# Half visits between turned scores, turned values a column later, and the last group's root and scaled rows placed otherwise

## The chip, the cores and the metric

One core of a Trainium2 chip. The metric is device time in microseconds of one execution, median of three runs.

## The reference

A layer on 16 sequences of 256 channels by 512 positions: cross attention over the channels (8 heads of 32 channels, softmax with a scale from each sequence's token count), a residual, layernorm, and a mixture of 8 experts with top-2 routing and a capacity of 1280 rows, with a second residual.

```python
s = SCALE * jnp.log(k_length.astype(jnp.float32))[:, None, None, None]
attn = jnp.einsum('bhdq,bhdk->bhqk', qh, kh)
attn = jax.nn.softmax(s * attn, axis=-1)
out = jnp.einsum('bhqk,bhdk->bhdq', attn, vh)
...
x = x + _L0_xcond_ref(_layernorm(x, axis=-1), ctx_2048, ctx_2048, itok_B_779_1933)
x = x + _L0_ffn_ref(_layernorm(x, axis=-1), L0_ffn_Wg, L0_ffn_w1, L0_ffn_w2)
```

The expert layer takes the softmax of `xr @ Wg`, its two largest values and their experts, counts each expert's rows in order, drops rows past the capacity, runs relu(x w1) w2 for each expert on its rows and adds the two results with their gates.

## The kernel before, in words

The attention works on 32 groups of 128 channels (4 heads each). Every engine has its own program, written out by hand; semaphores tie them together. The scores of a group are computed twice: unturned (queries on partitions, `ps_s`, L1050), from which VectorE takes the row maxima (`nmax`, L668), and turned (keys on partitions, `ps_t`, L1003), with the maxima as two more rows of the stack, from which ScalarE takes the exponentials (`probs`, L447). Queries and keys are split into a high and a low part (`qhi`, `khi` on ScalarE, L515 and L439; `qlo`, `klo` on GpSimd, L402 and L393), which SyncE stacks by DMA (`qst`, `kst`).

A step s is a software pipeline over groups: unturned scores of group s, turned scores of group s - 2, in 4 columns c of 4 heads i, one of each kind in turn. In between stand "half visits" (`weighted`): products of probabilities and values (`products`, `ps_o`, L971) and row sums (`row_sums`, `ps_l`, L979) for two chunks; chunks 2 and 3 of group s - 3 behind column 0, chunks 0 and 1 of group s - 2 behind column 2. Ahead of column 2 stand four transposes of the scaled rows of group s - 5 (`row_turned`, L1010) and four of the context, which give the values (`values`, L1018, of group s - 1). Both go into the turned scores' banks; ScalarE copies them out (`x2t` L494, `vt` L454). Behind column 3 come the router's logits. There are three banks of each kind: score k waits until score k - 3 has been read (`s_free`, `t_free`). `bank_turns` gives the number of each use of a bank.

In odd steps from 7 on a pair of groups is routed: VectorE, between its maxima, forms gates (`pr` L703, two inputs), the token numbers (`xrow<-tok` L709, one input), the indices of the two largest (`topi` L717), `hot` (L721, two inputs) and counts. GpSimd does in each step, in this order: the root of the next group's variance (`st` L377, L380, L385), `klo`, the residual addition (`x` L330, `residual`), in even steps four indirect writes of rows to the experts' buffer (`dispatch`, L336), `qlo`, and a second root (`root2`, L367, L370).

After the steps come the last two groups' turned scores (g = 30 and 31) with the half visits, the transposes and the logits in between, on four banks; then, for the last two groups, rows scaled (`x_scaled` L573), turned, logits, experts picked, counted (`places`), and written (`dispatch_one`). `warm` issues matmuls whose result is not used. When all rows are written, the experts start; their part is PE bound and is not touched.

SyncE's program asks for `ct` (context, L269) of group s + 3 after the values of group s - 1 have been turned:

```python
if g >= 4:
    sp.wait_ge(t_done, t_turn["vt", g - 4])
    sp.wait_ge(klo_ready, g - 3)
sp.dma_start(ct[g % 4][:], by_dim(ctx_rows, g)).then_inc(c_ld[g % 4], 16)
```

Of the kernel before, what the change touches and what calls it, by code (L numbers as in the profile page):

```python
# [10 lines left out]
ALU = mybir.AluOpType  # L11
# [55 lines left out]
def bank_turns():  # L67

    s_turn, t_turn = {}, {}
    for s in range(SLOTS):  # L70
        for c in range(NC4):
            if c == 2 and live(s - 5):
                t_turn["x2t", s - 5] = len(t_turn) + 1
            if c == 2 and live(s - 1):
                t_turn["vt", s - 1] = len(t_turn) + 1
# [27 lines left out]
def attention_and_dispatch(nc, x_rows, ctx_rows, klen, wg, out_rows, disp, totals, fill, spare,  # L103
                           w1, w2, raw, raw_ld, xin, first_ld, ident):
    s_turn, t_turn, (s_main, t_main) = bank_turns()
    with ExitStack() as stack:
# [201 lines left out]
        def _(pool):  # L308
# [31 lines left out]

            def dispatch(i):
# [9 lines left out]
                rows_to_experts(2 * i)  # L351
                rows_to_experts(2 * i + 1)
# [11 lines left out]

            def root2(g):
                pool.wait_ge(var2, g + 1)
                nc.gpsimd.tensor_scalar(st2[g % 2][:, 8:9], st2[g % 2][:, 7:8], EPS, None, ALU.add  # L367
                                        ).then_inc(veps2, 1)
                pool.wait_ge(veps2, g + 1)
                nc.gpsimd.tensor_tensor(st2[g % 2][:, 9:10], st2[g % 2][:, 8:9], nhalf[:], ALU.pow  # L370
                                        ).then_inc(rstd2, 1)
# [53 lines left out]
            root2(G - 1)  # L425
# [6 lines left out]
        def _(act):  # L432
# [48 lines left out]
            for s in range(-2, SLOTS):  # L481
                for c in range(NC4):
# [12 lines left out]
                    if c == 2 and live(s - 1):  # L495
                        values(s - 1)
                    for i in range(HPG):
                        if live(s - 2):
                            powers(s - 2, c, i)
                        if (c, i) == (0, 2) and pair_in(s):  # L500
# [4 lines left out]
                            for h in range(2):  # L505
                                nc.scalar.activation(lexp[:, h, :], lg[n % 2][:, h, :], ACT.Exp, bias=lmax[:, h:h + 1]
                                                     ).then_inc(rt["lexp"], 1)
                    if c == 0 and live(s - 3):
                        sums_out(s - 3)
                    if c == 1 and s >= 0 and live(s + 2):  # L510
                        keys_high(s + 2)
                    if live(s + 2) and c == (1 if s < 0 else 3):
# [9 lines left out]
            for g in (G - 2, G - 1):  # L522
                for c in range(NC4):
                    powers(g, c, 0)
                    powers(g, c, 1)
                    if c == 0:
                        sums_out(g - 1)
                        row_turned(g - 3)
# [18 lines left out]
        def _(dve):  # L547
# [84 lines left out]
            for s in range(-2, SLOTS):  # L632
# [28 lines left out]
                for c in range(NC4):  # L661
                    for i in range(HPG):
# [29 lines left out]
                        if (c, i) == (0, 1) and live(s + 2):  # L692
# [200 lines left out]
            x_scaled(G - 1)  # L893
# [3 lines left out]
            nc.vector.tensor_tensor(last[:, 1, :], last[:, 0, :], picked[:, 0, :], ALU.add).then_inc(rt["before"], 1)  # L897
            gates_found(B, G - 2, 0, 1)
# [28 lines left out]
        def _(pe):  # L927
# [55 lines left out]
            def last_weighted():  # L983
                pe.wait_ge(t_free, t_turn["t", G - 1, NC4 - 1, HPG - 1])
                held = probs[(NC4 * G - 1) % NPROBS]
                for h in range(HPG):
                    hd = slice(HD * h, HD * h + HD)
# [833 lines left out]
```

## Time and profile before

| | |
|---|---|
| median of 3 runs | 2154.31 us (2147.97, 2154.31, 2155.99) |
| the profiled execution | 2153.56 us, its span 2151.8 us |
| TensorE (PE) busy | 2087.6 us (97%) |
| weight loads (PEld) busy | 1511.5 us (70%) |
| VectorE (DVE) busy | 1032.1 us (48%) |
| ScalarE (ACT) busy | 679.6 us (32%) |
| GpSimd (POOL) busy | 472.7 us (22%) |
| VectorE busy, 60 to 560 us | 446.32 of 500 us |
| TensorE busy, 60 to 560 us | 496.56 of 500 us |
| experts, from about 650 us | 1501.8 us, TensorE busy 1485.14 |

The first scores start at 24 us and end at 584; the last two groups' turned scores run to 625, the dispatch to 640. The odd step shown below begins at 317.4, the even one at 299.9; step 31 begins at 566.7. A row of a timeline gives start and duration; the duration of a matmul is longer than the distance to the next one, because they overlap. In brackets stands how long the engine (or the weight load, PEld) was idle before, and what ended it.

### The profile page before, as it was taken

Reading aid. Unit: us, or ns where it says so; the run is one execution under the profiler, and the core shown is the slowest. Engines: PE = TensorE matmul, PEld = TensorE weight load, DVE = VectorE, ACT = ScalarE, POOL = GpSimd, SP = SyncE. Lnnn points to the kernel's source line nnn. Section 1 sums busy time; section 2 is a strip of 40 time slices with the busy share of each in tenths; the row PEclk is TensorE's granted clock in tenths of the full one; section 3 lists DMA queues with packets and bytes.
Section 4 is the critical chain, followed back from the end, with each engine's and each line's share of the span. In section 5 each row is a group of like instructions: output and inputs, shape, how many; then the busy total and the mean of one; then the engine's idle time right before and its main releaser. Section 6 shows DMA issues by size and latency. Waiting matters only on the chain. (4 is left out here: it accounts for less than half of the span.)

```text
span 2151.8 us, 26863 instructions
## 1 busy us (share of the span) xinstructions
PE 2087.6 (97%) x10150; PEld 1511.5 (70%) x10150; DVE 1032.1 (48%) x1914; ACT 679.6 (32%) x1187; POOL 472.7 (22%) x591
## 2 busy tenths in 40 slices
PE   3999999999989999999999999999999999999997
PEld 1455555555557788878888888888887788888775
DVE  5788989898844343233324324423332342333211
ACT  1666666666533132122213212312211231221110
POOL 3334444444332103010310301111031011101101
PEclk9999999999999999999999999999999999999999
DMA  9877778777545426125322613622532252241101
GB/s 148 168 165 183 173 184 179 182 178 179 107 152 145 96 82 140 21 42 128 70 38 83 136 21 80 132 45 40 128 69 41 60 132 45 40 128 29 20 3 20
DMA packets 177962, 215.89 MB, mean 100 GB/s; under 512 B 33807, under 2 KB 105487, under 8 KB 177808
## 3 DMA queue, kind: packets, MB, share of 16 engines
q1 hardware_dynamic: 154128, 173.21, 34.5%
q0 software_dynamic: 22240, 37.92, 9.2%
q10 hardware_dynamic: 1440, 2.70, 0.5%
q8 instruction: 97, 1.59, 0.3%
q14 instruction: 57, 0.47, 0.1%
HBM read 113.93 MB, written 68.29 MB: 85 GB/s over the span
## 5 line engine op out<-in xcount | busy, mean ns | idle before, releaser
L1551 DVE SCALAR_TENSOR_TENSOR hlo<-ps_h,hhi 128x512 fp32r<-128x512 f32 x256 | 177.2, 692 | 937.4 <-ACT hhi L1428 901.5
L1428 ACT ACTIVATE hhi<-ps_h 128x512 fp32r<-128x512 f32 x256 | 153.7, 600 | 1128.4 <-PE ps_h L1692 1114.9
L1690 PE MATMUL ps_h<-xhi,w1hi 128*128 128x512 f32 x1024 | 405.0, 396 | 2.2 <-PEq L1277 1.3
L1709 PE MATMUL ps_y<-w2hi,hhi 128*128 128x512 f32 x1024 | 404.0, 394 | 1.5 <-issue 0.8
L1710 PE MATMUL ps_y<-w2lo,hhi 128*128 128x512 f32 x1024 | 404.0, 395 | 1.4 <-issue 1.4
L1691 PE MATMUL ps_h<-xlo,w1hi 128*128 128x512 f32 x1024 | 404.7, 395 | 0.0
L1692 PE MATMUL ps_h<-xhi,w1lo 128*128 128x512 f32 x1024 | 404.3, 395 | 0.0
L1711 PE MATMUL ps_y<-w2hi,hlo 128*128 128x512 f32 x1024 | 403.9, 394 | 0.0
L668 DVE TENSOR_REDUCE nmax<-ps_s 128x1 f32<-128x512 f32 x512 | 328.9, 678 | 62.1 <-PE ps_s L1050 54.3
L447 ACT ACTIVATE probs<-ps_t 128x512 f32<-128x512 f32 x504 | 266.5, 613 | 133.0 <-PE ps_t L1003 129.5
L1690 PEld LDWEIGHTS ps_h<-xhi,w1hi 128*128 128x128 f32 x1024 | 192.6, 188 | 50.0 <-issue 3.9
L1711 PEld LDWEIGHTS ps_y<-w2hi,hlo 128*128 128x128 f32 x1024 | 192.2, 188 | 47.7 <-issue 1.6
L1709 PEld LDWEIGHTS ps_y<-w2hi,hhi 128*128 128x128 f32 x1024 | 192.2, 188 | 47.3 <-DVE hlo L1551 1.2
L1710 PEld LDWEIGHTS ps_y<-w2lo,hhi 128*128 128x128 f32 x1024 | 192.3, 188 | 47.1 <-issue 1.0
L1692 PEld LDWEIGHTS ps_h<-xhi,w1lo 128*128 128x128 f32 x1024 | 192.7, 188 | 46.3
L1691 PEld LDWEIGHTS ps_h<-xlo,w1hi 128*128 128x128 f32 x1024 | 192.7, 188 | 46.1
L1050 PE MATMUL ps_s<-kst,qst 96*128 96x512 f32 x416 | 185.4, 457 | 30.2 <-DMA qst<-qlo 27.3
L1363 POOL DMA_INDIRECT out_x<-y,ids x64 | 103.5, 1617 | 455.5 <-DVE y L1593 441.5
L1003 PE MATMUL ps_t<-qst,kst 98*128 98x512 f32 x408 | 165.6, 409 | 5.4 <-DMA qst<-nturn 2.4
L1345 POOL TENSOR_TENSOR ids<-xtail,zeros 128x4 int32<-128x4 int32 x15 | 5.2, 347 | 714.2 <-DMA xtail<-dispatched 714.2
L1050 PEld LDWEIGHTS ps_s<-kst,qst 96*128 96x128 f32 x416 | 81.6, 197 | 106.3 <-issue 64.9
L971 PE MATMUL ps_o<-probs,vt 128*32 128x512 f32 x1016 | 122.7, 600 | 1.8 <-ACT probs L447 1.8
(194 smaller groups left out, 1967.1 us busy)
## 6 DMA issues: line engine op xcount, KB each, us to landing
raw<-in_L_ffn_w SPq DMA_DIRECT2D x128, 512.0 KB
qst<-qhi SPq DMA_DIRECT2D x64, 256.0 KB, 7.5
xin<-dispatched SPq DMA_DIRECT2D x60, 256.0 KB, 5.9
kst<-khi SPq DMA_DIRECT2D x52, 256.0 KB, 6.4
xt<-in_x SPq DMA_DIRECT2D x32, 256.0 KB, 3.0
ct<-in_ctx SPq DMA_DIRECT2D x32, 256.0 KB, 4.2
qst<-qlo SPq DMA_DIRECT2D x32, 256.0 KB, 8.2
xres<-in_x SPq DMA_DIRECT2D x32, 256.0 KB, 4.5
```

The costliest lines, as they stand in the source:

```text
L447: nc.scalar.activation(probs[n % NPROBS][:, i, :], t_at(k)[:], ACT.Exp).then_inc(t_free, 1)
L668: nc.vector.tensor_reduce(nmax[s % 2][:, i, c:c + 1], s_at(k)[:], AX, ALU.max, negate=True).then_inc(s_free, 1)
L1003: nc.tensor.matmul(bank[:], kst[g % KR][0:STACK + 2, i, cols], qst[g % KR][0:STACK + 2, i, :], start=True, stop=True).then_inc(t_done, 1)
L1050: nc.tensor.matmul(bank[:], qst[s % KR][0:STACK, c, cols], kst[s % KR][0:STACK, c, :], start=True, stop=True).then_inc(s_done, 1)
L1428: nc.scalar.activation(hhi[k % 2][:], ps_h[k % 3][:], ACT.Relu).then_inc(hhi_ready, 1)
L1551: nc.vector.scalar_tensor_tensor(hlo[k % 2][:], ps_h[k % 3][:], 0.0, hhi[k % 2][:].bitcast(F32), ALU.max, ALU.subtract).then_inc(h_ready, 1)
L1690: nc.tensor.matmul(to, w1hi[:, c, fs], xhi[n % 2][:, c, :], start=(c == 0), stop=False)
L1691: nc.tensor.matmul(to, w1hi[:, c, fs], xlo[n % 2][:, c, :], start=False, stop=False)
L1692: done = nc.tensor.matmul(to, w1lo[:, c, fs], xhi[n % 2][:, c, :], start=False, stop=(c == NC4 - 1))
L1709: nc.tensor.matmul(ps_y[b][:], hhi[k % 2][:, bs], w2hi[:, f, :], start=(f == 0), stop=False)
L1710: nc.tensor.matmul(ps_y[b][:], hhi[k % 2][:, bs], w2lo[:, f, :], start=False, stop=False)
L1711: done = nc.tensor.matmul(ps_y[b][:], hlo[k % 2][:, bs], w2hi[:, f, :], start=False, stop=(f == NF - 1))
```

## The change

Nothing is computed otherwise; instructions change places.

- Values (`values` on TensorE and their copy on ScalarE) stand ahead of column 3 instead of column 2, and `bank_turns` with them.
- On ScalarE `keys_high(s + 2)` (khi) moves from behind column 1 to behind column 0, ahead of `sums_out`; `qhi` from behind column 3 to behind column 2.
- On VectorE `q_stats(s + 2)` moves from behind maximum (0, 1) to behind (0, 3).
- In the last two groups every column gets half a visit, between its second and third turned score: row sums of chunks 2 and 3 of the group before, their products, products of chunks 0 and 1, their row sums. Chunks 2 and 3 of the last group both stand in `last_weighted`.
- `root2(G - 1)` moves into the dispatch of groups 28 and 29, between them; `x_scaled(G - 1)` behind the counts; `row_turned(G - 1)` behind `places(B)`.

```diff
@@ bank_turns, ScalarE and TensorE alike
-            if c == 2 and live(s - 1):
+            if c == 3 and live(s - 1):
                 t_turn["vt", s - 1] = len(t_turn) + 1
...
@@ dispatch (GpSimd)
                 rows_to_experts(2 * i)
+                if i == B - 2:
+                    root2(G - 1)
                 rows_to_experts(2 * i + 1)
...
             dispatch(B - 2)
-            root2(G - 1)
             dispatch_one(G - 2)
...
@@ ScalarE, steps
+                    if c == 0 and s >= 0 and live(s + 2):
+                        keys_high(s + 2)
                     if c == 0 and live(s - 3):
                         sums_out(s - 3)
-                    if c == 1 and s >= 0 and live(s + 2):
-                        keys_high(s + 2)
-                    if live(s + 2) and c == (1 if s < 0 else 3):
+                    if live(s + 2) and c == (1 if s < 0 else 2):
...
@@ ScalarE, last two groups
                     if c == 0:
+                        row_turned(g - 3)
+                    if c == 1:
                         sums_out(g - 1)
-                        row_turned(g - 3)
...
@@ VectorE
-                        if (c, i) == (0, 1) and live(s + 2):
+                        if (c, i) == (0, 3) and live(s + 2):
                             q_stats(s + 2)
...
             experts_picked(B, lg[(B - 1) % 2], 0, 1)
-            x_scaled(G - 1)
             experts_marked(B, 0, 1)
...
             nc.vector.tensor_tensor(last[:, 1, :], last[:, 0, :], picked[:, 0, :], ALU.add).then_inc(rt["before"], 1)
+            x_scaled(G - 1)
             gates_found(B, G - 2, 0, 1)
...
@@ TensorE, last_weighted
+                g = G - 1
+                pe.wait_ge(t_free, t_turn["t", g, 2, HPG - 1])
+                row_sums(g, (2,))
+                products(g, (2,))
+                pe.wait_ge(t_free, t_turn["t", g, 3, HPG - 1])
+                row_sums(g, (3,)).then_inc(l_done, 1)
+                products(g, (3,)).then_inc(pv_done, 2)
...
@@ TensorE, last two groups
                     if c == 0:
-                        weighted(g - 1, (2, 3))
+                        pe.wait_ge(t_free, t_turn["t", g - 1, 3, HPG - 1])
+                        row_sums(g - 1, (2, 3)).then_inc(l_done, 1)
+                    if c == 1:
+                        products(g - 1, (2, 3)).then_inc(pv_done, 2)
                     if c == 2:
-                        weighted(g, (0, 1))
-                    if c == 3 and g == G - 1:
-                        weighted(g, (2,))
+                        pe.wait_ge(t_free, t_turn["t", g, 1, HPG - 1])
+                        pe.wait_ge(t_free, t_turn["vt", g])
+                        pe.wait_ge(o_saved, g)
+                        products(g, (0, 1))
+                    if c == 3:
+                        pe.wait_ge(l_saved, g)
+                        row_sums(g, (0, 1)).then_inc(pv_done, 2)
...
-            row_turned(G - 1)
             pe.wait_ge(rt["counted"], B - 1)
             pe.wait_ge(rt["picked"], B)
             places(B, 0, 1)
+            row_turned(G - 1)
```

How the instructions move, first on ScalarE in an odd step, from the routing's exponentials of column 0 on. Before:

```order
L506 ACTIVATE lexp<-lg,lmax 128x8 x2
L447 ACTIVATE probs<-ps_t 128x512
L460 ACTIVATE o_sb<-ps_o 128x512
L447 ACTIVATE probs<-ps_t 128x512 x4
L439 ACTIVATE khi<-ct 128x512
L494 ACTIVATE x2t<-ps_t 128x512
L454 ACTIVATE vt<-ps_t 128x512
L447 ACTIVATE probs<-ps_t 128x512 x8
L515 ACTIVATE qhi<-qf 128x512
L447 ACTIVATE probs<-ps_t 128x512 x4
```

Now (the changed kernel's lines are numbered one or two apart):

```order
L507 ACTIVATE lexp<-lg,lmax 128x8 x2
L448 ACTIVATE probs<-ps_t 128x512
L440 ACTIVATE khi<-ct 128x512
L461 ACTIVATE o_sb<-ps_o 128x512
L448 ACTIVATE probs<-ps_t 128x512 x4
L495 ACTIVATE x2t<-ps_t 128x512
L448 ACTIVATE probs<-ps_t 128x512 x4
L516 ACTIVATE qhi<-qf 128x512
L455 ACTIVATE vt<-ps_t 128x512
L448 ACTIVATE probs<-ps_t 128x512 x8
```

The copy of the keys has moved from between the exponentials of column 1 and `x2t` to ahead of `o_sb`, the copy of the values behind column 2, and `qhi` ahead of it.

TensorE in group 30, from its column 0 to column 2 (`ps_l` and `ps_o` rows are the half visits). Before:

```order
L1003 MATMUL ps_t<-qst,kst 128x512 x2
L979 MATMUL ps_l<-probs,ones 32x512 x8
L971 MATMUL ps_o<-probs,vt 32x512 x8
L1010 MATMUL ps_t<-ident,xrow 128x128 x4
L1003 MATMUL ps_s<-qst,kst 128x512
L1003 MATMUL ps_t<-qst,kst 128x512 x3
L1026 MATMUL ps_s<-wg_sb,qf 128x8 x4
L1003 MATMUL ps_s<-qst,kst 128x512
L1003 MATMUL ps_t<-qst,kst 128x512 x3
L971 MATMUL ps_o<-probs,vt 32x512 x8
L979 MATMUL ps_l<-probs,ones 32x512 x8
L1018 MATMUL ps_s<-ident,ct 128x32x4 x4
```

Now:

```order
L1001 MATMUL ps_t<-qst,kst 128x512 x2
L981 MATMUL ps_l<-probs,ones 32x512 x8
L1008 MATMUL ps_t<-ident,xrow 128x128 x4
L1001 MATMUL ps_s<-qst,kst 128x512
L1001 MATMUL ps_t<-qst,kst 128x512 x3
L973 MATMUL ps_o<-probs,vt 32x512 x8
L1024 MATMUL ps_s<-wg_sb,qf 128x8 x4
L1001 MATMUL ps_s<-qst,kst 128x512
L1001 MATMUL ps_t<-qst,kst 128x512 x3
L973 MATMUL ps_o<-probs,vt 32x512 x8
L1016 MATMUL ps_s<-ident,ct 128x32x4 x4
L1001 MATMUL ps_t<-qst,kst 128x512 x3
```

Where 16 matmuls of a visit stood together, 8 stand between each two pairs of turned scores; the row sums of chunks 0 and 1 follow further down, in column 3.

GpSimd at the end, from the dispatch of groups 28 and 29 (`rowi` of 4 columns) on. Before:

```order
L347 TENSOR_TENSOR rowi<-rowd,zeros 128x4
L336 DMA dispatched<-xrow,rowi 10240x528 x4
L367 TENSOR_SCALAR st_1<-st_1 128x1
L370 TENSOR_TENSOR st_1<-st_1,nhalf 128x1
L360 TENSOR_TENSOR rowi<-rowd,zeros 128x2
L336 DMA dispatched<-xrow,rowi 10240x528 x2
L360 TENSOR_TENSOR rowi<-rowd,zeros 128x2
L336 DMA dispatched<-xrow,rowi 10240x528 x2
```

Now:

```order
L355 TENSOR_TENSOR rowi<-rowd,zeros 128x4
L336 DMA dispatched<-xrow,rowi 10240x528 x2
L343 TENSOR_SCALAR st_1<-st_1 128x1
L346 TENSOR_TENSOR st_1<-st_1,nhalf 128x1
L336 DMA dispatched<-xrow,rowi 10240x528 x2
L370 TENSOR_TENSOR rowi<-rowd,zeros 128x2
L336 DMA dispatched<-xrow,rowi 10240x528 x2
L370 TENSOR_TENSOR rowi<-rowd,zeros 128x2
L336 DMA dispatched<-xrow,rowi 10240x528 x2
```

The two instructions of the last group's root have moved ahead of two of the four row writes.

## Rows read from the trace of the kernel before

**Rows 1.** Timeline of TensorE, odd step: start, duration, what, count
```profile
325.16 0.63 PE L1010 MATMUL ps_t<-ident,xrow 128*128 128x128 f32 x4
325.65 0.63 PE L1018 MATMUL ps_t<-ident,ct 128*128 128x128 f32 x4
...
328.70 1.92 PE L971 MATMUL ps_o<-probs,vt 128*32 128x512 f32 x16
```

**Rows 2.** Timeline of TensorE, an even step, and step 31
```profile
307.69 0.63 PE L1010 MATMUL ps_t<-ident,xrow 128*128 128x128 f32 x4
...
310.98 1.92 PE L971 MATMUL ps_o<-probs,vt 128*32 128x512 f32 x16
...
574.51 0.63 PE L1010 MATMUL ps_t<-ident,xrow 128*128 128x128 f32 x4
...
577.99 1.93 PE L971 MATMUL ps_o<-probs,vt 128*32 128x512 f32 x16
```

**Rows 3.** Timeline of the weight loads, odd step, with what ended the idle time
```profile
327.05 0.19 PEld L1003 LDWEIGHTS ps_t<-qst,kst 98*128 98x128 f32 x1 [0.50 <-ACT x2t L494]
...
328.04 0.19 PEld L1050 LDWEIGHTS ps_s<-xin,qst 96*128 96x128 f32 x1 [0.33 <-DVE nmax L668]
```

**Rows 4.** Timeline of VectorE, odd step
```profile
326.03 0.16 DVE L703 TENSOR_TENSOR pr<-lexp,zinv 128x16 f32<-128x16 f32 x1
...
326.38 0.15 DVE L709 TENSOR_SCALAR xrow<-tok 128x2 int32<-128x2 f32 x1
...
328.51 0.71 DVE L721 TENSOR_TENSOR hot<-e_f,topi 128x32 f32<-128x32 f32 x1
```

**Rows 5.** Timeline of GpSimd, odd step
```profile
325.52 0.19 POOL L385 TENSOR_TENSOR st<-st,sharp 128x1 f32<-128x1 f32 x1
326.65 1.28 POOL L393 TENSOR_TENSOR klo<-ct,khi 128x512 fp32r<-128x512 f32 x1 [0.94 <-ACT khi L439]
327.89 1.28 POOL L330 TENSOR_TENSOR x<-o_sb,xres 128x512 f32<-128x512 f32 x1
```

**Rows 6.** One line's instructions, L721: count, duration in ns, min/median/max
```profile
L721 DVE TENSOR_TENSOR hot<-e_f,topi x13: 186/717/731, 149.4 to 577.8; 128x32 f32<-128x32 f32 x13
```

**Rows 7.** Timelines of VectorE and GpSimd at the kernel's start
```profile
10.22 1.10 DVE L642 CAST tok<-tok_i 128x32 f32<-128x32 int32 x1
...
10.02 1.26 POOL L402 TENSOR_TENSOR qlo<-qf,qhi 128x512 fp32r<-128x512 f32 x1 [1.02 <-ACT qhi L515]
```

**Rows 8.** Timeline of TensorE, group 30, values behind a half visit
```profile
599.96 0.66 PE L1018 MATMUL ps_s<-ident,ct 128*128 128x128 f32 x4
600.37 0.95 PE L1003 MATMUL ps_t<-qst,kst 98*128 98x512 f32 x3
```

**Rows 9.** Timeline of TensorE, group 30, the visit with chunks 0 and 1
```profile
594.69 3.18 PE L971 MATMUL ps_o<-probs,vt 128*32 128x512 f32 x16 [1.28 <-ACT probs L447]
597.63 2.40 PE L979 MATMUL ps_l<-probs,ones 128*32 128x512 f32 x16
```

**Rows 10.** Busy time by stretch: length, PE, PEld, DVE, ACT, POOL, granted clock, DMA, GB/s
```profile
596.00:597.00 1.00, 1.00 (x12) 0.36 (x8) 0.00 (x0) 0.00 (x0) 0.00 (x0) 0.50 0.99 371
...
584.00:626.00 42.00, 36.94 (x255) 16.97 (x255) 20.57 (x79) 20.74 (x44) 13.50 (x21) 0.96 0.38 134
```

**Rows 11.** Timelines of VectorE, GpSimd and TensorE, last group's variance, root and rows
```profile
628.63 0.18 DVE L786 BATCH_NORM_AGGREGATE st<-st 128x2 f32<-128x6 f32 x1
...
630.20 0.25 POOL L367 TENSOR_SCALAR st<-st 128x1 f32<-128x1 f32 x1
...
631.74 0.66 PE L1010 MATMUL ps_t<-ident,xrow 128*128 128x128 f32 x4 [0.77 <-DVE xrow L573]
```

**Rows 12.** SyncE's load of ct, ScalarE's fourth exponential of the next step, landing of ct loads
```profile
314.21 0.62 SPq L269 DMA_DIRECT2D ct<-in_ctx  x1
...
320.29 0.59 ACT L447 ACTIVATE probs<-ps_t 128x512 f32<-128x512 f32 x1
...
DMA to landing us min/median/max: 3.0/4.2/4.7
```

More of the change, by code:

```diff
@@ L339, in rows_to_experts, with root2 @@
                         bounds_check=E * CAP - 1, oob_is_err=False).then_inc(row_st[g % RING], 16)
+            def root2(g):
+                pool.wait_ge(var2, g + 1)
+                nc.gpsimd.tensor_scalar(st2[g % 2][:, 8:9], st2[g % 2][:, 7:8], EPS, None, ALU.add
+                                        ).then_inc(veps2, 1)
+                pool.wait_ge(veps2, g + 1)
+                nc.gpsimd.tensor_tensor(st2[g % 2][:, 9:10], st2[g % 2][:, 8:9], nhalf[:], ALU.pow
+                                        ).then_inc(rstd2, 1)
             def dispatch(i):
@@ L363, in dispatch_one @@
                 rows_to_experts(g)
[L365 to L371, printed above, removed]
             for s in range(-2, SLOTS):
@@ L494, in _ @@
                         nc.scalar.activation(x2t[:], t_at(k)[:], ACT.Copy).then_inc(t_free, 1)
-                    if c == 2 and live(s - 1):
+                    if c == 3 and live(s - 1):
                         values(s - 1)
@@ L983, in last_weighted @@
             def last_weighted():
[L984 to L987, printed above, removed]
-                    done = nc.tensor.matmul(ps_l[hd, :], ones[:, 0:HD], held[:, h, :], start=False, stop=True)
-                done.then_inc(l_done, 1)
-                for h in range(HPG):
-                    hd = slice(HD * h, HD * h + HD)
-                    done = nc.tensor.matmul(ps_o[hd, :], vt[(G - 1) % 4][:, NC4 - 1, hd], held[:, h, :],
-                                            start=False, stop=True)
-                done.then_inc(pv_done, 1)
+                g = G - 1
[5 more added lines that the diff above has]
+                products(g, (3,)).then_inc(pv_done, 2)
             def turned_logits(g, c, i):
@@ L1041, in _ @@
                         row_turned(s - 5)
-                    if c == 2 and live(s - 1):
+                    if c == 3 and live(s - 1):
                         values(s - 1)
```

## The prediction, made before the changed kernel ran

> **What bounds the kernel now.** I read the page first, then the timeline engine by engine. The page has TensorE busy nearly throughout, and the reader should not take that for a floor: a busy matmul row also covers short waits for a bank. From about 650 us on the experts run, and the change does not touch them. So the question lies in the first 640 us: the 32 steps, the last two groups, and the dispatch after them.
>
> In an odd step (from s = 7 to 31, 13 of them, a pair of groups is routed as well) two transposes stand ahead of column 2 of the scores, and the products begin 3.54 us after the first of them (328.70 - 325.16) [rows 1]. In even steps the same stretch takes 3.29 us (310.98 - 307.69) [rows 2]. What the weight loads wait for tells why [rows 3]: a turned score waits 0.50 us for ScalarE, which still copies x2t, and the last unturned score waits 0.33 us for a maximum of VectorE. The second wait is a wall of its own: in step 31 no keys are copied ahead of x2t, and the stretch still takes 3.48 us (577.99 - 574.51) [rows 2].
>
> Next, VectorE and GpSimd side by side [rows 4, 5]. `hot` takes 0.71 us; its shortest run takes 0.19, its median 0.72 [rows 6]. It started inside the residual addition on GpSimd (327.89 to 329.17) and ended 0.05 us after it. At the kernel's start a VectorE cast of 32 elements with one input took 1.10 us and ended 0.04 us after `qlo` on GpSimd [rows 7]. So these VectorE instructions, begun while GpSimd runs a 512-wide addition or subtraction, wait for its end.
>
> **The change, part by part.**
>
> *Turned values one column later (TensorE).* Taken out of column 2 they free 0.49 us (325.65 - 325.16) [rows 1]. Behind a half visit they cost 0.41 us, by the one place where values follow products already (600.37 - 599.96) [rows 8]. In odd steps the wall stays where it was, so 0.41 is added: 13 x 0.41 = +5.3 us. In even steps at best 0.49 + 0.50 goes, with ScalarE's copy of the keys gone from ahead of x2t; laying out the maxima one behind the other, they let 0.55 through. Net -0.14 in each of 13, -1.8 us (0 to 13 x 0.58 = -7.5).
>
> *Key copy (khi) earlier on ScalarE.* It lands where ScalarE waits for the products ahead of `o_sb`; as work it costs nothing. But it releases GpSimd. Before, `klo` stood idle 0.94 us for khi and ran from 326.65 [rows 5]. Now khi is long there, and `klo` follows the small `st` product that ends at 325.71: it runs 325.71 to 326.99, and the residual addition, 1.24 later as before, 326.95 to 328.23. VectorE starts `pr`, with two inputs in SBUF like `hot`, at 326.03 [rows 4], 0.32 us after `klo`. It should end 0.05 after `klo`, at 327.04 instead of 326.19: 0.85 us late. Then comes `xrow<-tok`, with one input, 0.35 us after the start of `pr`: now at about 327.2, inside the residual addition. It would end at 328.27 instead of 326.53, 1.74 us late. Queued behind it are the maxima of (1,3) and (2,0), whose banks are the wall. `hot` is then free, but it stands behind these maxima. Price: 12 odd steps (step 31 has no keys) x 1.74 = +20.9 us. The bounds are 12 x 0.85 = +10.2 if only `pr` waits, and 0 if neither does. I take the upper one, because the nearest row for a one-input instruction is the cast of rows 7, and it waited.
>
> The Trainium skill, page "SBUF — State Buffer", section "SBUF: two separate sides", says that VectorE and GpSimd share a port pair under an exclusive lock, which VectorE needs for two SBUF inputs or for a two-port mode. By that rule `pr` waits; rows 6 agree for `hot`. The page "VectorE: DVE Perf Modes", section "What auto-detection actually checks", gives the two-port mode to one-source instructions from SBUF to SBUF with even outer dimensions, as `xrow<-tok` is; no row here shows that instruction beside a long GpSimd one. With this rule the term is 20.9, without it 10.2.
>
> *Clock.* With those waits TensorE stands still: it has done two pairs of column 2 by about 326.7 and may start the third unturned score at 328.9, when the maximum of (1,3) is over, 2.2 us later. The one stretch among the scores at 1.2 GHz (granted clock 0.50 [rows 10]) came after TensorE had waited 1.28 us [rows 9]. It made the first half of that visit take 3.18 us instead of 1.92 [rows 1, 9] and the second 2.40 instead of about 1.9: 1.75 us. It need not fall in every step; I take half of the 12: 6 x 1.75 = +10.5 us (0 to 21).
>
> *Half visits apart in the last two groups.* TensorE is idle 5.06 us between 584 and 626 (42.00 - 36.94) [rows 10], mostly for exponentials just ahead of a visit, 1.28 us the longest. With half a visit (one row of 16 matmuls, 1.92 us at full clock [rows 1]) between pairs of turned scores, ScalarE has its scores sooner and TensorE has work while it waits. Laying out both queues I keep half of the waits: -2.5 us (0 to -5.0). The number of switches between kinds of matmul stays. With the waits halved the slow stretch of rows 10 should go: -1.75 us (0 to -1.75).
>
> *Root and scaled rows of the last group.* Its variance is ready at 628.81, its root starts at 630.20, after four row writes [rows 11]. Placed after two, it can start 1.35 us sooner. But TensorE is busy until 0.77 us ahead of row_turned(31), and `places` now stands in front of it (about 0.3). -0.5 us (0 to -1.35). The two row writes behind the root start later; the last group's own writes still wait for its rows to be found, so this holds nothing up. x_scaled behind the counts costs nothing: it waits for the root anyway.
>
> *No effect.* q_stats two maxima later: the maxima whose banks TensorE needs keep the same instructions ahead of them. qhi earlier: ScalarE waits for products there. *A queue that slips:* SyncE's load of ct waits for turned values, so it is asked for not at 314.21 but at about 314.7, and lands within 4.7 us [rows 12], at 319.4; khi's turn comes after the exponential of 320.29, 1.4 us later. The loads behind it on SyncE (xres, the key and query stacks, and the store of x1) slip by as much; the stacks are for two steps on.
>
> **Sum:** 5.3 - 1.8 + 20.9 + 10.5 - 2.5 - 1.75 - 0.5 = +30.15 us on the profiled execution's 2153.56, which is 2183.7. The median of the runs lies 0.75 above that execution, so I say 2184.5. A measurement of this kernel can tell about 0.5%, 10.8 us, from no change.
>
> **Rivals.**
>
> *A: only `pr` waits.* For: `xrow<-tok` handles two elements, the cast 32. Against: the cast waited to the very end of `qlo`. Sum: 5.3 - 1.8 + 10.2 - 4.75 = +8.95, 2163, and up to 2169 with three or four slow-clock stretches. Chance 0.22.
>
> *B: no collision, so not slower.* It is decided by 0.32 us: if `klo` starts after 326.03, `pr` is through, and `hot` is late as before, behind the wall. Or a 16-wide `pr` is too small to be held. For: in the row shown it takes 0.16, and it has never met a long GpSimd instruction. Against: `hot` is 32 wide and its median run is held. Sum: 5.3 - 1.8 - 4.75 = -1.25, 2153. Chance 0.10.
>
> *C: the wall gives way.* The waits for x2t go in all 27 steps that have one, and VectorE keeps up: 27 x (0.41 - 0.49 - 0.50) - 4.75 = -20.4, 2134. Against: step 31. Chance 0.02.
>
> *D: late keys.* The load of ct lands more than 1.4 us late, khi waits and holds `o_sb` and column 1's exponentials. It decides from a landing time of 6.1 us; the longest is 4.7. At 1 us in each of 27 steps on top of the forecast: 2211 and over. Chance 0.03.
>
> **How the numbers follow.** The forecast has 0.63, and alone reaches from 2174 (no slow clock) to 2195 (slow clock in all 12). With A it is 0.85, so the range is 2162 to 2196. Slower by over 0.5%: the forecast, D, and a third of A, 0.74. Within: the rest of A and most of B, 0.23. Faster: C and a little of B, 0.03.
>
> **What would show it.** Right: in 12 odd steps `pr` near 1.0 us instead of 0.16 and `xrow<-tok` near 1.0 instead of 0.15; `hot` back at 0.19; no idle time of `klo` for khi; a wait of TensorE of 2 us ahead of the third score of column 2; odd steps longer by 2.15 us at full clock, even ones shorter by 0.1; a granted clock under 1 in parts of 100 to 560 us; idle time of TensorE in the last two groups about 2.6 us. Wrong: `pr` at 0.16 in the steps (B), `xrow<-tok` at 0.15 behind a long `pr` (A), or steps as long as before.

## The result, and the profile after

The changed kernel took 2175.41 us (median of 4 runs, 2172.08 to 2177.94) against 2153.32 us for the kernel before on the same chip (4 runs): a ratio of 1.0105, 95% interval 1.008 to 1.013. That is 22 us slower. The forecast was 2184.5 us, its range 2162 to 2196. The profiled execution took 2177.01 us with a span of 2175.3. On another chip the same kernel stood at 1.030 (last experiment), and that was not foreseen.

**The collision.** First the three instructions of VectorE that the prediction spoke of, in the profile after. Each row sums up all instructions of one line of the kernel (count, duration in ns as min/median/max, start of the first and the last):

```profile
L705 DVE TENSOR_TENSOR pr<-lexp,zinv x13: 167/952/960, 146.5 to 605.5; 128x16 f32<-128x16 f32 x13
L711 DVE TENSOR_SCALAR xrow<-tok x13: 151/1025/1027, 147.7 to 605.8; 128x2 int32<-128x2 f32 x13
L723 DVE TENSOR_TENSOR hot<-e_f,topi x13: 170/174/179, 150.7 to 607.9; 128x32 f32<-128x32 f32 x13
```

`pr` and the token write `xrow<-tok` went from 0.16 and 0.15 us to 0.95 and 1.03; `hot` went the other way, from 0.72 [rows 6] to 0.17. The timelines of VectorE, then of GpSimd, in an odd step of the profile after (start, duration) show what they stood beside:

```profile
339.42 0.95 DVE L705 TENSOR_TENSOR pr<-lexp,zinv 128x16 f32<-128x16 f32 x1
340.40 0.24 DVE L709 MAX8 top<-pr 128x8 f32<-128x8 f32 x2
340.56 1.02 DVE L711 TENSOR_SCALAR xrow<-tok 128x2 int32<-128x2 f32 x1
341.50 0.68 DVE L670 TENSOR_REDUCE nmax<-ps_s 128x1 f32<-128x512 f32 x1
...
339.05 1.28 POOL L395 TENSOR_TENSOR klo<-ct,khi 128x512 fp32r<-128x512 f32 x1
340.30 1.25 POOL L330 TENSOR_TENSOR x<-o_sb,xres 128x512 f32<-128x512 f32 x1
```

`pr` ended at 340.37, 0.04 us after `klo` (340.33); `xrow<-tok` ended at 341.58, 0.03 after the residual addition (341.55). So it is in all 12 odd steps: 0.02 to 0.04 us behind the end of the GpSimd instruction. `klo` has lost its wait for khi [rows 5], and starts 0.37 us ahead of `pr` (predicted 0.32). The two top-8 searches (MAX8) ran at full speed inside the residual addition: 0.24 us for both, as in the kernel before. The next maxima end late, and TensorE waits for one ahead of the third score of column 2:

```profile
342.23 0.50 PE L1048 MATMUL ps_s<-xin,qst 96*128 96x512 f32 x1 [1.93 <-DVE nmax L670]
```

There are 12 such waits between 149 and 571 us, all 1.93 to 1.95 us.

**The length of a step.** One reciprocal of the row sums (`r_few`, VectorE) stands in each step at the same place, so the distance between two is a step. Rows of the profile before, then of the profile after:

```profile
322.50 0.25 DVE L586 RECIPROCAL r_few<-l_turned 128x16 f32<-128x16 f32 x1
341.07 0.25 DVE L586 RECIPROCAL r_few<-l_turned 128x16 f32<-128x16 f32 x1
358.08 0.25 DVE L586 RECIPROCAL r_few<-l_turned 128x16 f32<-128x16 f32 x1
```

```profile
319.05 0.25 DVE L588 RECIPROCAL r_few<-l_turned 128x16 f32<-128x16 f32 x1
335.83 0.25 DVE L588 RECIPROCAL r_few<-l_turned 128x16 f32<-128x16 f32 x1
356.51 0.25 DVE L588 RECIPROCAL r_few<-l_turned 128x16 f32<-128x16 f32 x1
```

Before, a long and a short distance follow each other, here 18.57 and 17.01 us, and 18.64 and 17.02 mostly. After, the short one is 16.79 and the long one 20.68 us. The long one is the odd step with its routing work. Five of the eleven long ones between 143 and 565 us are 1.4 to 2.6 us longer still, and there the granted clock is at its lower level for a while. Busy time by stretch (length, PE, PEld, DVE, ACT, POOL, granted clock, DMA share, GB/s), first the kernel before, then the one after; its second and third rows are the microsecond behind a wait of TensorE, once with the fall of the clock and once without:

```profile
100.00:570.00 470.00, 467.02 (x2992) 244.69 (x2992) 421.92 (x987) 290.15 (x579) 207.89 (x322) 1.00 0.76 177
```

```profile
100.00:570.00 470.00, 446.61 (x2808) 229.57 (x2800) 404.96 (x929) 280.59 (x546) 195.52 (x306) 0.97 0.79 168
...
226.00:227.00 1.00, 1.00 (x3) 0.64 (x4) 1.00 (x3) 0.00 (x0) 0.00 (x0) 0.50 0.11 17
305.00:306.00 1.00, 0.87 (x4) 0.35 (x3) 1.00 (x2) 0.48 (x1) 0.00 (x0) 1.00 0.18 31
...
614.50:651.50 37.00, 35.56 (x257) 16.32 (x257) 20.37 (x79) 21.04 (x44) 14.28 (x22) 1.00 0.44 152
```

The last of these rows is the two last groups, cut at the same instructions as 584 to 626 us before: 1.44 us of idle time of TensorE in 37 us, where 42 us had 5.06 [rows 10], and no slow stretch. The idle time is three waits of 0.48 us, where there were eight of 0.36 to 1.28 [rows 9], for instance:

```profile
624.05 1.92 PE L973 MATMUL ps_o<-probs,vt 128*32 128x512 f32 x16 [0.48 <-ACT probs L448]
```

The last group's root no longer stands behind row writes: it starts when its variance is there.

```profile
654.37 0.22 POOL L343 TENSOR_SCALAR st<-st 128x1 f32<-128x1 f32 x1 [1.92 <-DVE st L788]
```

**Where the 22 us went**, by landmarks common to both traces: the first turned score of group 30 comes 30.56 us later, the last group's row_turned 25.47 (so the last two groups are 5.09 us shorter), the last row write 24.80 (0.67 shorter), the end of the span 23.5. The last 1.3 is the experts' start, where the stretch at the lower clock is shorter.

### The profile page after: what moved, and what is told of

The parts are those of the page before. It is cut to its first block and busy times, and to the rows that moved or that the text cites. A ratio compares the mean times of both kernels' runs of the same rounds, so it can differ in the third digit from the quotient of the medians.

```text
span 2175.3 us, 26863 instructions
## 1 busy us (share of the span) xinstructions
PE 2092.7 (96%) x10150; PEld 1511.2 (69%) x10150; DVE 1040.0 (48%) x1914; ACT 687.7 (32%) x1187; POOL 472.0 (22%) x591
## 5 line engine op out<-in xcount | busy, mean ns | idle before, releaser
L448 ACT ACTIVATE probs<-ps_t 128x512 f32<-128x512 f32 x504 | 270.9, 608 | 70.0 <-PE ps_t L1001 67.3
L1048 PE MATMUL ps_s<-kst,qst 96*128 96x512 f32 x416 | 190.9, 470 | 47.7 <-DMA qst<-qlo 27.3
L973 PE MATMUL ps_o<-probs,vt 128*32 128x512 f32 x1024 | 128.9, 623 | 1.0 <-ACT probs L448 1.0
```

Source lines behind the costliest of these rows:

```text
L448: nc.scalar.activation(probs[n % NPROBS][:, i, :], t_at(k)[:], ACT.Exp).then_inc(t_free, 1)
L1048: nc.tensor.matmul(bank[:], qst[s % KR][0:STACK, c, cols], kst[s % KR][0:STACK, c, :], start=True, stop=True).then_inc(s_done, 1)
```

## The experiments

**1. Only khi put back.** The changed kernel, with khi behind column 1 again:

```diff
-                    if c == 0 and s >= 0 and live(s + 2):
-                        keys_high(s + 2)
                     if c == 0 and live(s - 3):
                         sums_out(s - 3)
+                    if c == 1 and s >= 0 and live(s + 2):
+                        keys_high(s + 2)
```

> The change with one part undone: khi (the copy of the keys) is again behind column 1 on ScalarE. Theory (the two instructions of VectorE held by klo and the residual addition are the loss): pr back at 0.16 us and xrow<-tok at 0.15, no stretch of granted clock 0.5 in the steps, long steps 18.64 + 0.41 = about 19.0 us instead of 20.68, and the kernel 20.9 + 9.6 (the slow stretches) = some 30 us less in the steps minus the x2t wait that returns in 26 steps (up to 0.5 us each in the even ones, 6.5 in all): 2145 to 2153 us. Rival (the turned values standing a column later are the loss): the time stays within 5 us of 2175 and the long steps stay near 20.7 us. Rival on the clock (the slow stretches come from the new order of TensorE's work, not from its wait): the time falls by some 15 to 20 us only and stretches at 0.5 remain between 100 and 570 us.

Measured: 2150.31 us, ratio to the kernel before 0.9997 (0.9988 to 1.0007). In one line's instructions:

```profile
L705 DVE TENSOR_TENSOR pr<-lexp,zinv x13: 162/164/168, 147.3 to 578.3; 128x16 f32<-128x16 f32 x13
L723 DVE TENSOR_TENSOR hot<-e_f,topi x13: 182/714/726, 149.8 to 580.8; 128x32 f32<-128x32 f32 x13
```

The long step is 19.02 us, the short one 16.93, and the granted clock is 1.00 in all steps. So the whole loss of the changed kernel hangs on khi's place. What is left against the kernel before is +0.38 us in a long step and -0.09 in a short one, and it cancels against the gain at the end. The +0.38 is the price of the turned values a column later (experiment 5 has it with nothing else moved). The -0.09 isn't shown to be theirs: `q_stats` and `qhi` are moved here too.

**2. Only khi moved.** The kernel before, with khi behind column 0 and no other edit:

```diff
+                    if c == 0 and s >= 0 and live(s + 2):
+                        keys_high(s + 2)
                     if c == 0 and live(s - 3):
                         sums_out(s - 3)
-                    if c == 1 and s >= 0 and live(s + 2):
-                        keys_high(s + 2)
```

> The kernel before with one part of the change alone: khi behind column 0 on ScalarE. Theory: pr near 1.0 us and xrow<-tok near 1.0 us in 12 odd steps, odd steps 1.7 us longer, some stretches at granted clock 0.5; the x2t wait is gone, which gives up to 0.5 us in each of 13 even steps. Sum +20.9 - 6.5 + 0 to 20 (clock): 2167 to 2188 us. Rival (the collision costs only together with the values a column later, since those put two more maxima ahead of the banks that column 2 needs): pr and tok are long but the time stays within 5 us of 2153.

Measured: 2172.34 us, ratio 1.0104 (1.0087 to 1.0121), the same as the whole change.

```profile
L703 DVE TENSOR_TENSOR pr<-lexp,zinv x13: 165/952/960, 145.3 to 594.9; 128x16 f32<-128x16 f32 x13
```

```profile
335.52 0.50 PE L1050 MATMUL ps_s<-xin,qst 96*128 96x512 f32 x1 [1.62 <-DVE nmax L668]
```

The long step is 20.31 us (+1.67, and +1.66 in the changed kernel over experiment 1), the short one 16.64 (-0.38, as the x2t wait is gone: 0.5 us at most, 23 times between 140 and 570 us before, none here), and five stretches of lower clock stand in the steps. One edit gives the loss, its undoing takes it away.

**3. One of the two held instructions moved out of the way.** The changed kernel with the token write behind the counts in column 2:

```diff
                             for h in range(2):
                                 nc.vector.max(top[:, h, :], pr[:, h, :]).then_inc(rt["top"], 1)
-                            g = s - 7
-                            nc.vector.tensor_scalar(xrow[:, g % RING:g % RING + 2, IDCOL].bitcast(I32),
-                                                    tok[:, g:g + 2], 1.0, None, ALU.mult)
...
                             nc.vector.tensor_tensor(b_next[:, 0, :], b[:, 1, :], picked[:, 1, :], ALU.add
                                                     ).then_inc(rt["counted"], 1)
+                            g = s - 7
+                            nc.vector.tensor_scalar(xrow[:, g % RING:g % RING + 2, IDCOL].bitcast(I32),
+                                                    tok[:, g:g + 2], 1.0, None, ALU.mult)
```

> The change with the write of the token numbers (xrow<-tok, VectorE) moved from behind pr in column 1 to behind the counts in column 2, where GpSimd's residual addition is over. Theory (each of the two held instructions has its own price, 0.85 us for pr and 0.89 more for tok): pr stays near 0.95 us, tok is back at 0.15, the long step is 0.8 to 0.9 us shorter (20.68 to about 19.8), and the stretches of slow clock, which came after waits of over 1 us, are fewer or gone: 10.7 + 0 to 9.6 less, 2155 to 2165 us. Rival (whatever follows pr is held in its place, for instance the top-8 searches or the maximum of (1,3)): the time stays within 3 us of 2175. Rival (pr alone is harmless, tok alone is the price): the time falls by 20 us or more with the clock, to 2150 or less.

Measured: 2168.19 us, ratio 1.0083 (1.0066 to 1.0100). Rows of one odd step, on VectorE and on TensorE:

```profile
334.04 0.96 DVE L705 TENSOR_TENSOR pr<-lexp,zinv 128x16 f32<-128x16 f32 x1
...
337.95 0.16 DVE L741 TENSOR_SCALAR xrow<-tok 128x2 int32<-128x2 f32 x1
```

```profile
335.91 0.50 PE L1048 MATMUL ps_s<-xin,qst 96*128 96x512 f32 x1 [1.00 <-DVE nmax L670]
```

The long step at full clock is 19.72 us, 0.96 less (expected 0.8 to 0.9): the price of the token write, and of `pr` 0.70 (19.72 - 19.02). The split is a little uncertain, since the write's own 0.15 us has also gone from ahead of the maxima. Where it was moved without a collision (`parity_tok` against `parity`, below) that alone was worth 0.08. The rest of the expectation failed. Waits of 1.0 us instead of 1.94 brought not fewer slow stretches but more, 7 instead of 5, each some 1.6 us. In the traces the steps end 9.4 us sooner than in the changed kernel (first turned score of group 30 at 605.95 instead of 615.37), which is 11.5 less some 2 for the slow stretches. The medians, each against the kernel before in its own job, give only 4.7 us; no run shows where the rest is.

**4. Only the last part of the change.** The kernel before with half visits apart, root, scaled rows and row_turned as in the change, the steps untouched:

```diff
                     if c == 0:
-                        weighted(g - 1, (2, 3))
+                        pe.wait_ge(t_free, t_turn["t", g - 1, 3, HPG - 1])
+                        row_sums(g - 1, (2, 3)).then_inc(l_done, 1)
+                    if c == 1:
+                        products(g - 1, (2, 3)).then_inc(pv_done, 2)
...
             dispatch(B - 2)
-            root2(G - 1)
```

> The kernel before with the last part of the change alone: half visits between turned scores in the last two groups, the last group's root two row writes earlier, x_scaled behind the counts and row_turned behind the last places. The steps are as before. From the landmarks of the two traces: the last two groups 5.1 us shorter (1.75 of it the slow stretch in group 30, which goes), the dispatch 0.7 us shorter, and perhaps 1.7 us at the start of the experts (slow stretch 3.4 instead of 6.8 us long): 5.8 to 7.5 us less than the kernel before, 2146 to 2148 us. Rival (the last groups were shorter only because they were entered later, with the keys' and rows' transfers further on): within 2 us of the kernel before.

Measured: 2146.44 us, ratio 0.9982 (0.9972 to 0.9991). The last row write of the dispatch is issued at 633.31 us instead of 639.56, 6.25 sooner (5.8 expected); of that the medians show 4.5 (1.9 to 6.0 by the interval). This version is faster than both kernels, if by less than the 0.5% that one comparison tells: the interval lies below 1 here and in its repetition (experiment 7).

**5 and 6. Four kernels on another chip.** These four ran on a chip on which the kernel before took 2158.1 us, 7 more than on that of experiments 1 to 4. `values_alone` is the kernel before with the turned values in column 3 (in the table of turns, on ScalarE and on TensorE):

```diff
-                    if c == 2 and live(s - 1):
+                    if c == 3 and live(s - 1):
                         values(s - 1)
```

> The kernel before with the turned values a column later and nothing else. Theory (the terms of the prediction, +0.41 us in an odd step and -0.14 in an even one; undo_khi, which has them too, showed odd steps of 19.02 us against 18.63 and even ones of 16.93 against 17.02): odd steps 19.0 us, even ones 16.9, in sum +3.5 to +4 us over the kernel before, some 2154.5 us, no stretch of slow clock in the steps. Rival (the lengths of undo_khi come from q_stats and qhi, which it also moves): odd steps stay at 18.6 and even ones at 17.0, within 1 us of the kernel before.

Measured: 2173.62 us, ratio 1.0082 (1.0067 to 1.0098), 19 us over the expectation, 12 if the slower chip is allowed for. The long steps are 19.0 to 19.15 us and the first short one 17.09, near the expectation. The other short steps are not: 17.8 to 19.5 us. The place is the end of an even step, where TensorE computes the logits and VectorE copies them out. Rows of an undisturbed step, then of a late one:

```profile
174.87 0.95 PE L1069 MATMUL ps_s<-wg_sb,x2t 128*128 128x8 f32 x8
176.11 0.17 DVE L758 COPY lg<-ps_s 128x8 f32<-128x8 f32 x1
...
247.98 0.96 PE L1069 MATMUL ps_s<-wg_sb,x2t 128*128 128x8 f32 x8
250.26 0.17 DVE L758 COPY lg<-ps_s 128x8 f32<-128x8 f32 x1 [1.17 <-PE ps_s L1050]
```

The copy starts 2.28 us after the logits' first matmul instead of 1.24, with VectorE idle for it. In this trace it is 0.9 to 1.0 us late in 10 even steps in a row, from 213 us on. khi stands behind column 1 here, as in the kernel before.

`klo_behind_pr` is the changed kernel with khi early, but with GpSimd held until `pr` is through:

```diff
                     pool.wait_ge(khi_ready, g + 1)
+                    if pair_in(s):
+                        pool.wait_ge(rt["pr"], (s - 7) // 2 + 1)
                     nc.gpsimd.tensor_tensor(klo[g % 2][:], ct[g % 4][:], khi[g % 2][:].bitcast(F32), ALU.subtract
```

(the token write stands ahead of `pr` there, so that neither of the two meets a long GpSimd instruction).

> The change as it is, khi behind column 0 included, but GpSimd's klo waits in odd steps for pr, and VectorE writes the token numbers ahead of pr, so that neither meets a long GpSimd instruction. Theory (the loss is GpSimd's instruction running, not khi's place in ScalarE's queue): pr and tok at 0.16, the long steps near 18.7 to 19.1 us, short ones 16.8, no slow clock in the steps: 2144 to 2150 us. Rival (khi ahead of o_sb makes ScalarE late in odd steps, and the long pr only stood beside that): the long steps stay at 20 us and more, 2165 us or above. In between: klo, now later, meets hot, which is held 0.7 us or more behind the maxima that column 2 needs; that costs up to 0.5 us in 12 steps.

Measured: 2193.06 us, ratio 1.0165 (1.0138 to 1.0193).

```profile
L710 DVE TENSOR_TENSOR pr<-lexp,zinv x13: 167/169/172, 147.2 to 615.9; 128x16 f32<-128x16 f32 x13
L725 DVE TENSOR_TENSOR hot<-e_f,topi x13: 181/485/492, 149.6 to 618.3; 128x32 f32<-128x32 f32 x13
```

In the odd steps the theory held: with `pr` at 0.17 us the long step is 19.0 to 19.1 us, as with khi undone, although khi is as early as in the change. So it is GpSimd's running instruction that costs, not ScalarE's order. But the even steps are 17.6 to 22.3 us.

`parity` was to beat both kernels: experiment 4, with khi behind column 0 in even steps alone; `parity_tok` moves the token write as well.

```diff
-                    if c == 1 and s >= 0 and live(s + 2):
+                    if c == (1 if pair_in(s) else 0) and s >= 0 and live(s + 2):
                         keys_high(s + 2)
```

> A version that should beat both: the kernel before with the last part of the change (half visits apart, root, scaled rows) and with khi behind column 0 in even steps alone, where VectorE has no pr; in odd steps it stays behind column 1. Turned values stay in column 2. Theory: even steps 16.64 us as in khi_alone (17.02 before), odd ones 18.63 as before, no slow clock: 13 x 0.38 = 4.9 us less than tail_alone, 2141 to 2142 us. Rival (what an even step gains by the x2t copy coming sooner, the odd step behind it gives back, since VectorE's maxima set the pace): odd steps near 19.0 and the time within 1 us of tail_alone.

> As parity, and the write of the token numbers moved behind the counts in column 2. Theory (in odd steps the last unturned score of column 2 waits 0.33 us for a maximum, and the token write of 0.15 us stands ahead of it on VectorE): odd steps up to 0.2 us shorter, 18.45, so 12 x 0.2 = up to 2.4 us less than parity. Rival (the x2t copy or the maximum two places on takes the wait over): odd steps stay at 18.6 and the two are equal.

Measured: 2168.21 us, ratio 1.0050 (1.0038 to 1.0062), and 2170.31 us, 1.0064 (1.0051 to 1.0077). Both missed by over 25 us, some 20 if the slower chip is allowed for. The odd steps are 18.65 to 18.75 and 18.57 to 18.9 us, near the expectation; the even ones reach 22 and 21 us. (The profiled execution of `parity` took 2178.37 us, the longest of its six.)

**What is late in these even steps.** In `parity`, around column 3 of an even step (timeline of TensorE, VectorE and ScalarE):

```profile
282.81 0.50 PE L1048 MATMUL ps_s<-kst,qst 96*128 96x512 f32 x1
...
284.80 1.39 DVE L670 TENSOR_REDUCE nmax<-ps_s 128x1 f32<-128x512 f32 x2 [2.96 <-PE ps_s L1048]
284.84 0.60 ACT L448 ACTIVATE probs<-ps_t 128x512 f32<-128x512 f32 x1 [4.74 <-PE ps_t L1001]
285.55 0.50 PE L1048 MATMUL ps_s<-kst,qst 96*128 96x512 f32 x1 [1.05 <-issue]
```

The first score of column 3 is recorded at 282.81; its maximum, which starts 0.54 us after the score in every odd step of this trace, starts 1.99 us after it, and ScalarE's exponential is as late. Two engines that wait for TensorE alone are served 1.4 us late, so it is TensorE's results that are late, whatever its recorded starts say (they are modelled). In `parity` these delays are 0.7 or 1.4 to 1.5 us in 10 even steps from 205 us on, and a stretch at the lower clock follows each of them. `values_alone` has its first results of column 3 on time (0.51 us in every step); its delay stands behind that column.

**7. The same on a third chip**, with experiment 4 beside them (the kernel before: 2156.9 us).

> tail_alone once more, beside parity and klo_behind_pr, because those two ran on another chip than tail_alone did, one on which even the kernel before took 2158.1 us instead of 2150.9, and in their even steps TensorE's results came 1.3 us late in column 3 for no reason that the trace names. Theory X (the late results belong to that chip or to its transfers, not to the variants): on whichever chip this runs, tail_alone stands to parity as khi_alone's even steps say, parity 4 to 5 us faster. Theory Y (khi early in even steps brings the late results): tail_alone has even steps of 17.0 us and no late results beside a parity that has them.

> Theory X (the chip): if the kernel before takes about 2151 here, parity has even steps of 16.64 and odd ones of 18.63 to 18.75 us and takes 2141 to 2143 us. Theory Y (khi early in even steps): even steps of 17.3 to 22 us as on the other chip, 2160 us or more.

> Theory X (the chip): odd steps 19.0 to 19.1 us, as on the other chip, even ones 16.8, no slow clock in the steps, 2147 to 2152 us, some 24 us less than the change. Theory Y: even steps of 17.6 to 22 us again and 2175 us or more.

Measured: `tail_again` 2153.74 us, ratio 0.9984 (0.9974 to 0.9994), with long steps of 18.62 and short ones of 17.0 to 17.6; `parity_again` 2170.65, 1.0058 (1.0040 to 1.0076); `klo_behind_pr_again` 2195.16, 1.0174 (1.0125 to 1.0222). Here, with one chip for all three, theory Y holds for column 3: late results there come with khi early in even steps. It is not the whole story, since `values_alone` had its late results with khi late. And experiment 2 had khi early in even steps, and every queue's instructions at the same distances from column 3 (row writes 2.43 and 1.01 us ahead of its first score, 0.26 and 1.54 behind it), and short steps of 16.64 us throughout. So the order of the instructions alone doesn't bring the delay. Whether the rest belongs to the chip or to something else that differs from job to job is not shown, as each chip had one job.

**8. The changed kernel on another chip.**

> The changed kernel itself once more. On two other chips parity, whose even steps have every queue's instructions around column 3 where khi_alone has them (GpSimd's row writes 2.43 and 1.01 us ahead of column 3's first score, the third 0.26 behind it), had first results of column 3 0.7 or 1.4 us late in 10 even steps, khi_alone on its chip never. Theory X (those late results come with the chip, for any kernel whose khi is early in even steps): if the kernel before takes 2156 to 2158 us here, the change shows them too, even steps of 17.5 to 21 us instead of 16.79, and takes 2185 us or more, a ratio of 1.013 or above; if it takes about 2151, the change takes about 2175 with even steps of 16.79 throughout. Theory Z (they need odd steps without the long pr, that is TensorE without a wait in the odd step before): on a chip where before takes 2156 to 2158, the change has even steps of 16.8 all the same and a ratio of 1.010 to 1.011.

Measured: 2217.76 us (2215.39 to 2225.21) against 2154.9 for the kernel before (between the two cases that the expectation named), ratio 1.0299 (1.0270 to 1.0329). `pr` and `xrow<-tok` have the durations of the first profile (medians 951 and 1026 ns), and the shortest long step is 20.79 us. The short steps are 17.4 to 21.2 us, where they were 16.79. Column 3 of an even step here, and in the first profile of the same kernel (TensorE's first score, the turned values copied by ScalarE, the maximum of VectorE, SyncE's load, which waits for the turned values):

```profile
215.80 0.47 PE L1048 MATMUL ps_s<-kst,qst 96*128 96x512 f32 x1
...
217.61 0.62 SPq L269 DMA_DIRECT2D ct<-in_ctx  x1
217.62 0.60 ACT L455 ACTIVATE vt<-ps_t 128x512 f32<-128x512 f32 x1 [3.01 <-PE ps_t L1001]
217.65 1.29 DVE L670 TENSOR_REDUCE nmax<-ps_s 128x1 f32<-128x512 f32 x2 [3.11 <-PE ps_s L1048]
```

```profile
327.98 0.47 PE L1048 MATMUL ps_s<-kst,qst 96*128 96x512 f32 x1
...
328.26 0.62 SPq L269 DMA_DIRECT2D ct<-in_ctx  x1
328.26 0.60 ACT L455 ACTIVATE vt<-ps_t 128x512 f32<-128x512 f32 x1 [1.49 <-PE ps_t L1016]
...
328.49 1.29 DVE L670 TENSOR_REDUCE nmax<-ps_s 128x1 f32<-128x512 f32 x2 [1.78 <-PE ps_s L1048]
```

Three engines are served 1.8 us after the score's start instead of 0.3 to 0.5. Through all of it the granted clock is 1.00:

```profile
215.80:217.30 1.50, 1.42 (x8) 0.85 (x6) 0.00 (x0) 0.00 (x0) 1.11 (x2) 1.00 0.73 179
```

It falls only behind the delay. Eleven even steps between 175 and 592 us have it, by 0.5 to 1.4 us, and with the clock behind it they add some 33 us; the odd steps add 7 by more slow stretches. Of this expectation theory Z has fallen: the late results come behind odd steps with the long `pr` too. Theory X (the same kernel is late on one chip and not on another) fits. But the time of the kernel before, 2154.9 against 2153.3 on the first chip, doesn't tell in advance where the delay comes. What holds TensorE's results back is open. The row writes and loads are issued at the same distances on both chips, the DMA share in half-microsecond stretches is alike until the delay begins, and no fetch of instructions stands at those places in particular. No run took the row writes or the stack loads away to see.

## Why the prediction was right, and where not

- **The collision** was the main term (+20.9 us by 12 x 1.74) and stood as written: both instructions held, each to within 0.05 us of the end of the GpSimd instruction, `hot` free, step 31 untouched. By experiments 1 and 2 it costs 1.66 us a step, so 19.9. The token write, for which I had only a cast of 32 elements as evidence, has the larger share (0.96 against 0.70, or 0.88 against 0.78 if its own work is taken off). Rival A (`pr` alone) gave 10.2 for this term; experiment 3, which is rival A built, has the collision at 0.70 x 12 = 8.4.
- **The values a column later**: +0.41 an odd step was forecast, +0.38 measured. For even steps -0.14 was forecast; the change has -0.23 (13 x -0.23 = -3.0 instead of -1.8). The forecast took the gain by the early khi and the loss by the values together, as this measurement does.
- **The clock**: +10.5 by 6 of 12 steps at 1.75; five stretches of the long steps hold 9.5 us (237.0 in eleven, less 11 x 20.68). That the sum was right is luck in part: half of the 12 was a guess, and single stretches cost 1.4 to 2.6 us. The reason, that the lower clock comes with TensorE's waits, is borne out by experiments 1 and 2 (none without the waits, five with waits of 1.62 us), but experiment 3 shows that shorter waits need not bring fewer stretches.
- **The last two groups**: -4.25 was forecast for both terms, -5.09 came. Of the waits of TensorE more went than half: 1.44 us idle instead of the 2.6 forecast, so 3.6 us less where 2.5 was put. This term was sized too small.
- **Root and scaled rows**: -0.5 forecast, -0.67 measured. The experts' start, -1.3, was not in the sum, since its slow stretch belongs to a part that the change does not touch.
- **The sum** for the steps was 34.9 and the landmark says 30.56: each part came out a little smaller (collision 1.0, clock 1.0, even steps 1.2, odd ones 0.4; 0.7 is left over). So the forecast stood 9 us above the median, inside its range, and 22 us is beyond the 10.8 that counts as slower.
- **What failed** is the assumption behind the range that one chip stands for all. On the last chip the time, 2217.8, lies outside 2162 to 2196, by a delay of TensorE's results in even steps. The profile before has no such delay in column 3. It has one of 0.5 us, once, at the start of an odd step (the first maximum 1.30 us after its score, at 211.19 us, instead of 0.82), and nothing told that it could grow.

Rivals B (no collision) and C (the wall gives way) fell with the first rows; D (late keys) too, as `klo` shows no wait for khi.

The Trainium skill, page "VectorE: DVE Perf Modes", section "What auto-detection actually checks", lets a one-source instruction like `xrow<-tok` take the two-port mode. That it was held fits this, with 1.03 us instead of 0.15 for two elements; the trace doesn't name the mode. The MAX8 searches beside the same GpSimd instruction were not held (0.24 us for two).

## What to carry to other kernels

Before an instruction is taken forward on one engine, look what it releases on GpSimd, and which short VectorE instructions from SBUF to SBUF start inside that. The two-input ones (`pr`, `hot`) and the one-input `xrow<-tok` then last to the end of the GpSimd instruction, 0.7 to 1.0 us here for 0.16 us of work, 12 times; MAX8 does not. It is harmless where no bank is waited for behind it (`hot` before), and costs in full where one is. Keep the parts of such a change apart, since here a gain at the end (0.2%) was hidden under a loss in the steps (1.0% by experiment 2), and time a reordering on more than one chip before it is called good or bad.

## What was not expected of the hardware

- The same program stood at 1.0105 and at 1.0299 to the kernel before in two jobs on different chips, with the medians of the kernel before within 0.35% in all five jobs (2150.9 to 2158.1 us).
- TensorE's results came late at one place of a step, mostly by 0.5 to 1.5 us, at a granted clock of 1.00, for all who waited for them. The place was column 3 of even steps in six profiles, and the logits behind it in `values_alone` (0.9 to 1.0 us).
- Waits of TensorE of 1.0 us were followed by the lower clock in 7 of 12 steps, waits of 1.94 us in 5 of 12, and waits of 1.62 us in 5 of 12 (experiments 3 and 2 and the first profile): how long it waited does not tell by itself.
